# Loading the K weights of a fused attention and feed-forward layer in quarters instead of halves

## The reference

```python
q, k, v = (split_heads(x @ W.T + b) for W, b in ((Wq, bq), (Wk, bk), (Wv, bv)))
logits = einsum(k, Wrf) - 0.5 * sum(k * k)
alpha = softmax(logits over sequence and features)      # per head
N, D = einsum(alpha, v), sum(alpha)
phi = softmax(einsum(q, Wrf), features)
x = layernorm(x + (einsum(phi, N) / (einsum(phi, D) + eps)) @ Wo.T + bo)
e = argmin over 8 experts of a loss of mean(x), mean(x * x)
ffn = x @ base_W.T + conv_e(up_e(relu(down_e(x))))      # biases left out here
out = layernorm(x + ffn)
```

## Time and profile before

| what | us |
|---|---|
| median of the runs shown (2 runs) | 626.36 |
| the two runs | 624.33 and 628.39 |
| the profiled execution | 624.9 |
| its span on the slowest core (core 6) | 623.1 |
| spans of the eight cores | 606.0 to 623.1 |

### The profile page before, as it was taken

One profiled execution on the slowest core, in us unless ns is written; L12 is line 12 of the kernel. 1 busy time (PEld: TensorE's weight loads), 2 busy tenths in 40 slices (PEclk: granted clock), 3 DMA queues, 4 the chain that ended last, 5 costly groups with the idle time before them and its releaser, 6 DMA issues.

```text
span 623.1 us, 8705 instructions; the slowest of 8 cores (606.0 to 623.1 us)
## 1 busy us (share of the span) xinstructions
PE 470.0 (75%) x2816; PEld 236.7 (38%) x2855; DVE 254.7 (41%) x645; ACT 227.8 (37%) x728; POOL 26.7 (4%) x54
## 2 busy tenths in 40 slices
PE   0689999997787776877676486595687658888984
PEld 0234444444444436666332142242343224333331
DVE  3000024445666663223204152552637772355553
ACT  0123310004556664332524263462646202333233
POOL 2020000000000000000201011010000000000000
PEclk9989999999999997685887697795989968999998
DMA  7759542007000006162598775954919100022222
GB/s 97 115 99 157 102 77 58 1 1 136 1 2 1 2 2 109 36 103 51 76 150 145 120 118 95 161 96 92 167 28 177 46 1 1 35 101 102 103 101 101
DMA packets 10428, 49.26 MB, mean 79 GB/s; under 512 B 1917, under 2 KB 3072, under 8 KB 7889
## 3 DMA queue, kind: packets, MB, share of 16 engines
q0 software_dynamic: 6864, 38.12, 37.0%
q1 hardware_dynamic: 3522, 10.60, 4.6%
HBM read 77.38 MB, written 9.45 MB: 139 GB/s over the span
## 4 chain that ended last, share of the span: by engine, by line
PE 46%; DMA 24%; DVE 11%; ACT 11%; issue 6%; POOL 1%; DVEq 0%; ACTq 0%; POOLq 0%
DMA scr<-wuaug 14%; PE pb L320 8%; PE pb L279 6%; PE pb L459 5%; PE pb L1031 5%; DMA xstg<-xtok 4%; DMA axA<-xT 4%; PE pb L354 4%; ACT scr L390 2%; ACT scr L395 2%; PE pb L581 2%; PE pb L551 2%; DMA wg<-wk 2%; PE pb L413 1%; PE pb L714 1%
## 5 line engine op out<-in xcount | busy, mean ns | idle before, releaser
L390 ACT ACTIVATE scr<-pb,mxb 128x64 bf16<-128x64 f32 x128 | 42.2, 330 | 94.7 <-DVE mxb L385 94.7
L279 PE MATMUL pb<-axA,wg 128*128 128x512 bf16 x220 | 57.3, 400 | 24.4 <-DMA axA<-xT 23.9
L714 PE MATMUL pb<-wg,axD 128*128 128x512 bf16 x243 | 62.9, 402 | 12.4 <-DVE ddbuf L656 5.9
L459 PE MATMUL pb<-wg,scr 128*65 128x512 bf16 x112 | 37.1, 487 | 41.3 <-DMA scr<-wuaug 34.4
L1031 PE MATMUL pb<-wg,axC 128*128 128x512 bf16 x234 | 55.4, 378 | 8.6 <-ACT iostg L1073 8.3
L667 ACT ACTIVATE axD<-pb,ddbuf 128x64 bf16<-128x64 f32 x128 | 46.7, 384 | 22.3 <-DVE ddbuf L656 21.9
L320 PE MATMUL pb<-wg,axA 128*128 128x512 bf16 x220 | 53.4, 379 | 0.3
L354 PE MATMUL pb<-axA,wg 128*128 128x512 bf16 x215 | 52.3, 379 | 1.4 <-DVE axC L327 1.1
L673 ACT ACTIVATE axD<-pb,ddbuf 128x64 bf16<-128x64 f32 x128 | 47.3, 390 | 0.0
L284 ACT ACTIVATE axD<-pb,smallsb 128x512 bf16<-128x512 f32 x32 | 22.0, 687 | 60.4 <-PE pb L276 59.4
L279 PEld LDWEIGHTS pb<-axA,wg 128*128 128x128 bf16 x224 | 22.6, 102 | 53.5 <-issue 29.9
(11 more groups left out here) (169 smaller groups left out, 734.7 us busy)
## 6 DMA issues: line engine op xcount, KB each, us to landing
wg<-wct POOLq DMA_DIRECT2D x8, 2048.0 KB, 16.5
out<-iostg SPq DMA_DIRECT2D x16, 512.0 KB, 2.6
axA<-xT POOLq DMA_DIRECT2D x4, 1024.0 KB, 13.5
wg<-wk POOLq DMA_DIRECT2D x2, 1024.0 KB, 10.5
wg<-wv POOLq DMA_DIRECT2D x1, 2048.0 KB, 28.7
wg<-wq POOLq DMA_DIRECT2D x1, 2048.0 KB, 14.8
wg<-wo POOLq DMA_DIRECT2D x1, 2048.0 KB, 15.5
xstg<-xtok POOLq DMA_DIRECT2D x8, 256.0 KB, 11.5
```

Source lines behind the costliest of these rows:

```text
L279: st=(kc == 0): t.matmul(o, a, b, start=st, stop=False))
L390: sc.activation(o, i_, AF.Exp, bias=b, scale=1.0))
L459: st=(kc == 0): t.matmul(o, a, b, start=st, stop=False))
L714: st=(kc == 0): t.matmul(o, a, b, start=st, stop=False))
```

## The change

The load of Wk is cut into four quarters of 2048 columns (0.5 MB of bf16 each) instead of two halves. The first quarter goes out with the first chunk of x. GpSimd then waits for every quarter before it issues the next, and for the last quarter before it issues the second chunk of x. Two semaphores are added (`gxb`, `gxc`). TensorE waits for the second quarter ahead of group 2, the third ahead of group 4, the fourth ahead of group 6. No computation changes.

```diff
-        emi("gpsimd", lambda g: g.dma_start(wg[:, 0:4096], wk[:, 0:4096]), "g1", 16)
+        emi("gpsimd", lambda g: g.dma_start(wg[:, 0:2048], wk[:, 0:2048]), "g1", 16)
         emi("gpsimd", lambda g: g.dma_start(axA[:, 0:4096], xT[:, 0:4096]), "g1", 16)
         wait("gpsimd", "g1", cnt["g1"])
-        emi("gpsimd", lambda g: g.dma_start(wg[:, 4096:8192], wk[:, 4096:8192]),
+        emi("gpsimd", lambda g: g.dma_start(wg[:, 2048:4096], wk[:, 2048:4096]),
             "gx", 16)
         wait("gpsimd", "gx", cnt["gx"])
+        emi("gpsimd", lambda g: g.dma_start(wg[:, 4096:6144], wk[:, 4096:6144]),
+            "gxb", 16)
+        wait("gpsimd", "gxb", cnt["gxb"])
+        emi("gpsimd", lambda g: g.dma_start(wg[:, 6144:8192], wk[:, 6144:8192]),
+            "gxc", 16)
+        wait("gpsimd", "gxc", cnt["gxc"])
         emi("gpsimd", lambda g: g.dma_start(axA[:, 4096:8192], xT[:, 4096:8192]),
             "xq1", 16)
...
+            if i == 2:
+                wait("tensor", "gx", gx_all)
             if i == 4:
-                wait("tensor", "gx", gx_all)
+                wait("tensor", "gxb", gxb_all)
+            if i == 6:
+                wait("tensor", "gxc", gxc_all)
             if i == 8:
                 wait("tensor", "xq1", xq1_all)
```

More of the change, by code:

```diff
@@ L129, in build_program @@
         for k in ("pe", "sc", "ve", "sd", "gp", "g0", "ga", "gb",
-                  "gc", "gw", "g1", "gx", "xq1", "xq2", "xq3", "g2", "s0",
+                  "gc", "gw", "g1", "gx", "gxb", "gxc", "xq1", "xq2", "xq3",
+                  "g2", "s0",
                   "sx0", "sx1", "sx2", "sx3", "so0", "so1", "sm", "sm2", "sm3"):
@@ L134, in build_program @@
                    gc=0, gw=0, g1=0, gx=0, xq1=0, xq2=0, s0=0, sx0=0, sx1=0,
-                   so0=0, so1=0, sm=0, sm2=0, sm3=0, xq3=0, g2=0, sx2=0, sx3=0)
+                   so0=0, so1=0, sm=0, sm2=0, sm3=0, xq3=0, g2=0, sx2=0, sx3=0,
+                   gxb=0, gxc=0)
         opsq = {k: [] for k in ("tensor", "scalar", "vector", "sync", "gpsimd")}
@@ L197, in build_program @@
         gx_all = cnt["gx"]
+        gxb_all = cnt["gxb"]
+        gxc_all = cnt["gxc"]
         g2_all = cnt["g2"]
```

## The result

The median of the changed kernel is 631.2 us (14 runs, 626.41 to 639.4) against 623.5 for the kernel before (13 runs). Two of the 14 ran in a slower state of the chip (636.62 and 639.4), so the ratio, here and in all later comparisons, is that of the fast runs alone: 1.0107, with a 95% interval from 1.0073 to 1.0141. The change makes the kernel about 1.1% slower, or 6.7 us: within the 2% that the prediction counted as no change, but clear of zero.

A forecast was written before the change was run, and what follows sets the result against it. The prediction took serialized loads up to chunk 1's landing as the K stage's bound: 6.5 us from added turns, 0 from the clock, on 624.9 gives 631.4, forecast as a median of 632.0 us, range 626.8 to 637.2.

The forecast's parts named there:

- The bound: K stage up to group 8: serialized loads bind, and group 8 starts at chunk 1's landing, 40.88 us before the change.
- The first load: First K-stage load, 1.5 MB instead of 2 MB: 3.2 us shorter, range 2.6 to 3.8.
- A quarter alone: A 0.5 MB load of Wk in the K stage: 6.1 us, range 4.8 to 6.9.
- the straight line: Estimate for a quarter of Wk, drawn between 4.8 us for 0.25 MB and 9.5 for 1 MB: 6.4 us.
- The string: Serialized K-stage loads with two more turns: chunk 1 lands at 47.4 us, 6.5 later, range 2.0 to 9.5.
- The clock: TensorE's slow pace after waiting ahead of group 8: already paid, so 0 added; up to 3 us more possible.
- Carried to the end: Stages behind the K stage: its 6.5 us lag reaches the end of the kernel undiminished.
- The sum: Whole kernel: 624.9 + 6.5 = 631.4 us, forecast as a median of 632.0, about 1% slower.
- The split pays: Rival at chunk 1's landing: a quarter under 3.9 us makes it land earlier; about 622 us, chance 0.04.
- The lag is absorbed: Rival behind the K stage: a later stage's reserve takes up the whole shift; 625 to 627 us, chance 0.10.
- The first load hardly shortens: Rival at the first load: it loses nothing, chunk 1 lands 9.7 us later; 635.4 us, chance 0.08.
- The clock costs more: Rival on TensorE: groups 8 to 10 all run at the lower clock, 3 us on top; 635 us, chance 0.08.

The follow-up runs named there:

- The late start: Changed kernel, but TensorE waits for the first three quarters of Wk ahead of group 0; ratio 1.0104 to the kernel before.
- first profile of before: The kernel before, no edit, in the profiled execution that the prediction was made from; it took 624.9 us.
- second profile of before: The kernel before, no edit, profiled again to see how steady its later stages are; ratio listed as 1.
- the warm-up: Changed kernel without GpSimd's waits between loads, plus 56 unused TensorE matmuls on zeros ahead of group 0; ratio 0.9926 to the kernel before.
- second run: Changed kernel with GpSimd's waits between loads removed, so all quarters are issued at once, measured a second time; ratio 0.9990 to the kernel before.

## Why the prediction was right, and where its terms were off

The forecast was 632.0 us and +1%; measured were 631.2 and +1.07%. Point by point:

- *The bound.* Right. Chunk 1's landing sets group 8: all eight cores wait 4.3 to 5.9 us for it, and the early start is hidden under that wait. The late start bears it out: giving up 12.5 us cost 2.3 at group 8, and that came back in the tail.
- *The first load.* 3.2 us shorter was forecast, 3.06 measured.
- *A quarter alone.* 6.1 us was forecast. It takes 6.33, 5.50 and 5.04 on the slowest core, 5.62 in the mean, and 5.0 on the four quick cores. The term was mis-sized: I split 9.5 into 3.0 fixed and 6.5 of transfer by reading off a gap in one-microsecond windows, and three sizes give 1.9 and 7.6 on the slowest cores, 2.4 and 5.1 on the quick ones. The gap that I took stands ahead of chunk 1 of x, whose first bytes move 2.3 us after the issue (windows of 0.1 us, core 6). Ahead of the half of Wk on the same core it was 1.3, and ahead of the three quarters 1.2 to 1.6 (core 4, changed kernel). The 4.8 us that the straight line started from was too long as well: 0.25 MB alone take 3.77.
- *The string.* Chunk 1 was to land 6.5 us later and lands 4.6 later from slowest core to slowest core, 4.5 in the mean of the cores (group 8 at 44.0 against 39.6, the mean of the two profiles of before). The three quarters make 1.4 of the 1.9 us missing, and chunk 1's own load, 8.81 instead of 9.42, the rest. On core 5, with quick loads in both profiles, it lands 6.1 later.
- *The clock.* This is the step that failed. I counted 0, because the slowest core already paid about 1.4 us ahead of group 8 and I held that to be the state of affairs. In the first profile of before only core 6 paid it (tail 43.48; the others have 42.15 or 42.16), in the second four cores did; in the changed kernel all eight do, with tails of 43.7 to 44.7. In the mean of the cores that is 44.3 against 42.6, 1.6 us. That two slow groups instead of one could follow was in my range, not in my sum.
- *Carried to the end.* Right, and now shown, within an interval from 4.8 to 9.9 us, by an edit that does nothing but delay: 6.9 us put in, 7.4 out.
- *The sum.* 4.5 us by the string and 1.6 by the clock make 6.1 of the 6.7 measured. I had 6.5 and 0. The total was right by luck, because two errors cancel, one in each term. The level of 632.0 had a third: it starts from about 625.5 for the kernel before, whose median over 13 runs is 623.5.
- *The rivals.* "The split pays" is out; a quarter would have had to take 3.9 us. "The lag is absorbed" is out. "The first load hardly shortens" is out. "The clock costs more" was partly true, at half its price, and holds together with the forecast's own mechanism rather than instead of it.

## What to carry to other kernels

Where loads are issued one behind the landing of the other, count turns before bytes. A turn cost 2.9 to 3.0 us here, and two more of them 4.6 us on the slowest core and 6.1 on one with quick loads. Finer pieces brought the K stage's end forward only when they were in flight together, and the time was clear of the kernel before only with the warm-up on top. An earlier start of an engine is worth nothing while the last gate of the stage stays where it is; on TensorE it can cost, since the idle time moves behind the first work and the matmuls after it run slow again. A slow restart that exists already on one core in one profile is not a constant: look at all cores, and at a second execution, before counting it as paid.

## What the runs showed of the hardware that I had not expected

- Whether TensorE restarts slowly is not fixed for idle times near 2 us. Ahead of group 8 it went on at the full pace after 2.19 us (core 4, first profile of before) and restarted at the lower level after 2.14 us (core 7, second profile of before). After 3.29 us and more ahead of group 8 it restarted at the lower level in every profile, and the tail was 1.4 to 2.9 us longer.
- Matmuls on a tile of zeros, their result unused, are enough to end the slow start: on six of eight cores groups 0 and 1 then ran at the full pace.
- The granted clock in the profile does not show the slow start of groups 0 and 1, only the later one. On core 6, first profile of before, it reads 1.00 from 21.00 to 24.38, where seven matmuls take 3.15 us, and 0.55 from 41.00 to 44.00, where they take 2.99. The pace of the matmuls has to be read beside it.
- With ten loads issued behind it, the first pair still lands at 18.6 us, where it lands at 17.9 with nothing queued behind it; in the mean of the cores, the later ones cost the first 0.7 to 1.0 us (two runs). The loads came in nearly in the order of their issue: on core 0 (second run) at 21.2, 24.4 and 27.5 for the quarters and 34.3, 40.2 and 47.3 for the chunks of x, and only Wv (60.1) landed behind a small load that was issued after it (59.9).
- With all eight cores loading at once, a load of 1 MB took 7.4 to 7.6 us on one core of each pair and 8.8 to 9.0 on the other (changed kernel, chunk 1).
- Whether a gain at the K stage's end shows in the time as a loss does stays open: about 7 us later gave 7.4 us, 5 us earlier gave about 1 in two comparisons and 4.6 in the third, the one with the warm-up.
